# Second attention: k projections written to the PSUM bank of output and routing, the router's logits one double step later

## The reference

```python
x = x + attn_a(layernorm(x), ...)   # 16 heads of 8, unit-norm q and k
x = x + ffn(layernorm(x), ...)      # 8 experts, top 2, capacity 384
x = x + attn_b(layernorm(x), ...)   # 16 heads of 64, position bias, output projection
x = x + ffn(layernorm(x), ...)

# attn_b, the part at issue
q = (h @ Wq).reshape(B, S, 16, 64)
k = (h @ Wk).reshape(B, S, 16, 64)
v = (h @ Wv).reshape(B, S, 16, 64)
probs = softmax(einsum('bqhd,bkhd->bhqk', q, k) / 8 + position_bias)
y = einsum('bhqk,bkhd->bqhd', probs, v).reshape(B, S, 1024) @ Wo

# ffn, its router
probs = softmax(layernorm(x) @ w_router)      # 8 experts
gate, expert = top_k(probs, 2)                # then the place of each token in its expert's rows
```

## Time and profile before

| what | us |
|---|---|
| median of 3 runs | 1679.59 |
| lowest and highest | 1674.07, 1686.88 |
| the profiled execution | 1677.58 |
| its span, first to last instruction | 1675.9 |
| PE busy | 1346.1 (80%) |
| ACT busy | 923.5 (55%) |
| DVE busy | 879.9 (53%) |
| POOL busy | 522.0 (31%) |

### The profile page before, as it was taken

How to read it: one execution, slowest core, us unless ns; L and a number is a source line. 1 busy time by engine, 2 the same in 40 slices (tenths; PEclk the granted TensorE clock), 3 DMA queues, 4 the chain that set the end, 5 groups by cost and what they waited for, 6 DMA issues and landing times. The chain is left out here.

```text
span 1675.9 us, 22605 instructions
## 1 busy us (share of the span) xinstructions
PE 1346.1 (80%) x6711; PEld 596.6 (36%) x6711; DVE 879.9 (53%) x2700; ACT 923.5 (55%) x1844; POOL 522.0 (31%) x789
## 2 busy tenths in 40 slices
PE   2388988887629179999999999999999999997374
PEld 1123333332117023343343343343433433432253
DVE  2445556553311046657667657667577576674211
ACT  0277777776404047656666656666566666564031
POOL 4100222222224413233423433422433334224235
PEclk9699999999859679999999999999999999998687
DMA  3335555556129213333323333323333232333062
GB/s 71 82 83 124 114 117 116 114 119 127 22 76 310 27 41 100 96 87 111 94 82 108 108 94 109 105 78 97 94 108 95 74 107 84 91 101 95 7 153 24
DMA packets 126889, 161.22 MB, mean 96 GB/s; under 512 B 36414, under 2 KB 80909, under 8 KB 126768
## 3 DMA queue, kind: packets, MB, share of 16 engines
q1 hardware_dynamic: 99376, 119.80, 27.5%
q0 software_dynamic: 27392, 39.98, 10.6%
HBM read 61.75 MB, written 36.09 MB: 58 GB/s over the span
## 5 line engine op out<-in xcount | busy, mean ns | idle before, releaser
L1247 POOL DMA_DIRECT2D crossed<-blocks x512 | 252.3, 501 | 609.4 <-DVE blocks L1514 543.8
L1503 DVE CUSTOM_DVE_ANT_0 tile<-s_ps,bias 128x512 f32<-128x512 f32 x512 | 331.2, 684 | 79.7 <-PE s_ps L1313 49.2
L1431 ACT ACTIVATE tile<-tile,low 128x512 f32<-128x512 f32 x512 | 363.2, 715 | 2.2 <-DVE low L1503 2.2
L632 ACT ACTIVATE probs_a<-score_ps,gbound 128x1024 f32<-128x1024 f32 x256 | 268.3, 1114 | 134.2 <-PE score_ps L861 134.1
L1423 ACT ACTIVATE pT<-p_ps 128x512 f32<-128x512 f32 x256 | 152.3, 595 | 269.0 <-PE p_ps L1321 267.3
L1313 PE MATMUL s_ps<-kT,qT 64*128 64x512 f32 x1024 | 255.1, 616 | 0.0
L1336 PE MATMUL o_psb<-pT,v_b 128*64 128x512 f32 x512 | 237.0, 606 | 6.8 <-DMA crossed<-blocks 6.8
L1336 PE MATMUL o_psb<-crossed,v_b 128*64 128x512 f32 x512 | 237.0, 606 | 0.0
L1321 PE MATMUL p_ps<-ident,tile 128*128 128x128 f32 x1024 | 164.6, 283 | 23.0 <-ACT pT L1423 22.9
L1321 PEld LDWEIGHTS p_ps<-ident,tile 128*128 128x128 f32 x1024 | 107.2, 140 | 207.9 <-issue 110.8
L1514 DVE STREAM_TRANSPOSE blocks<-tile 128x512 f32<-128x512 f32 x256 | 180.9, 707 | 0.3 <-ACT tile L1431 0.3
(11 more groups left out here) (153 smaller groups left out, 1484.9 us busy)
## 6 DMA issues: line engine op xcount, KB each, us to landing
crossed<-blocks SPq DMA_DIRECT2D x512, 64.0 KB, 2.6
crossed<-blocks POOLq DMA_DIRECT2D x512, 64.0 KB, 2.4
inv_row<-inv_rows SPq DMA_DIRECT2D x128, 128.0 KB, 2.9
k_stack<-k_parts SPq DMA_DIRECT2D x96, 96.0 KB
q_stack<-q_parts SPq DMA_DIRECT2D x96, 96.0 KB
bias_skew<-bias_rows SPq DMA_DIRECT2D x8, 1024.0 KB, 12.5
w_f<-in_w SPq DMA_DIRECT2D x32, 256.0 KB, 5.5
bias<-bias_skew SPq DMA_DIRECT2D x16, 448.0 KB, 12.4
```

Source lines behind the costliest of these rows:

```text
L632: nc.scalar.activation(probs[q % 2][:, c % 4, :], score_ps[c % 2][:, :], ACT.Exp, bias=gbound[:, :]).then_inc(p_ready.sem, 1)
L1247: pool.dma_start(strip_to(n, a, m), strip_from(n, a, m)).then_inc(crossed_sw[n % 2], 16)
L1431: nc.scalar.activation(tile[k % RING][s][:, :], tile[k % RING][s][:, :], ACT.Exp, bias=low[n % 2][:, s, i:i + 1], scale=-1.0, accum_out=su ...
L1503: nc.vector.tensor_tensor_reduce(out=tile[k % RING][s][:, :], in0=s_ps[k % 2][s][:, :], in1=bias[:, h, off:off + S], scale=1.0, scalar=3.0e38,
```

## The change

In the second attention k projections are written to `r_ps` instead of `m_ps`, and ACT copies them from there. The k projection no longer waits for the copy of q. The q projection and the v projections wait for the last q copied (odd counts of `qk_ready`), not for k. Since `r_ps` now has more users, waits are added on PE: k of pair 0 waits for PLACE of the batch two back, k of pair 3 for the residual, k of pairs 5 and 6 for TURNED and SHIFTED, and the output projection, the router's turn, logits and counts wait for k copies of the next batch. In `ROUTE` `logits` and `shift` go from 24 to 25, `exps` from 25 to 26, `pick` from 26 to 27; the rest stays. Numbers of instructions are the same.

```diff
@@ -1140,8 +1140,8 @@
         def tiles(t):
             return t.rearrange("p (t e) -> p t e", e=E_N)
 
-        ROUTE = dict(stats=20, rows=22, turn=(23, 1), copy=23, logits=(24, 1), shift=24,
-                     exps=25, pick=26, runs=28, counts=(29, 1), take=29, address=30)
+        ROUTE = dict(stats=20, rows=22, turn=(23, 1), copy=23, logits=(25, 1), shift=25,
+                     exps=26, pick=27, runs=28, counts=(29, 1), take=29, address=30)
         R_STEPS = range(20, 31)
 
         def since(eng, signal, b, k):
@@ -1289,19 +1289,25 @@
                 if m == 0:
                     wait(pe, xT_ready, b, 1)
                 else:
-                    wait(pe, qk_ready, b, {1: 2, 3: 4, 4: 6, 5: 8, 6: 10, 7: 12}.get(m, 2))
+                    wait(pe, qk_ready, b, {3: 3, 4: 5, 5: 7, 6: 9, 7: 11}.get(m, 1))
                     wait(pe, v_ready, b, m)
                 i, half = m % TB, m // TB
                 nc.tensor.matmul(m_ps[:, :], xT[:, i * P:(i + 1) * P], wv[:, half * S:(half + 1) * S],
                                  start=True, stop=True).then_inc(v_ps.sem, 1)
 
             def project(b, n, part):
-                if part == 1:
-                    wait(pe, qk_ready, b, 2 * n + 1)
+                if part == 0:
+                    wait(pe, v_ready, b, {0: 1, 1: 3, 2: 4, 3: 5, 4: 6, 5: 7, 6: 8, 7: 8}[n])
+                    since(pe, qk_ready, b, 2 * n - 1)
                 else:
-                    wait(pe, v_ready, b, {0: 1, 1: 3, 2: 4, 3: 5, 4: 6, 5: 7, 6: 8, 7: 8}[n])
                     since(pe, qk_ready, b, 2 * n)
-                nc.tensor.matmul(m_ps[:, :], (wq, wk)[part][:, n * P:(n + 1) * P], xT[:, :],
+                    if n == 0 and b >= 2:
+                        wait(pe, r.step, b - 2, r.PLACE)
+                    if n == 3 and b >= 1:
+                        wait(pe, res_done, b - 1, 1)
+                    if n in (5, 6) and b >= 1:
+                        wait(pe, r.step, b - 1, {5: r.TURNED, 6: r.SHIFTED}[n])
+                nc.tensor.matmul((m_ps, r_ps)[part][:, :], (wq, wk)[part][:, n * P:(n + 1) * P], xT[:, :],
                                  start=True, stop=True).then_inc(qk_ps.sem, 1)
 
             def scores(b, k):
@@ -1339,7 +1345,9 @@
 
             def output(b):
                 wait(pe, ctx_ready, b, PAIRS)
-                if b >= 1:
+                if b + 1 < B:
+                    wait(pe, qk_ready, b + 1, 6)
+                else:
                     wait(pe, r.step, b - 1, r.PLACE)
                 for i in range(TB):
                     for n in range(PAIRS):
@@ -1377,11 +1385,11 @@
 
             def routing(b, d, part):
                 if (d, part) == ROUTE["turn"]:
-                    r.turn(pe, b, turned, lambda: wait(pe, res_done, b, 1))
+                    r.turn(pe, b, turned, lambda: wait(pe, qk_ready, b + 1, 10) if b + 1 < B else wait(pe, res_done, b, 1))
                 elif (d, part) == ROUTE["logits"]:
-                    r.logits(pe, b, logits, lambda: None)
+                    r.logits(pe, b, logits, lambda: wait(pe, qk_ready, b + 1, 12) if b + 1 < B else None)
                 elif (d, part) == ROUTE["counts"]:
-                    r.counts(pe, b, counts, lambda: None)
+                    r.counts(pe, b, counts, lambda: wait(pe, qk_ready, b + 1, 16) if b + 1 < B else None)
 
             for d in range(LEAD, LAST):
                 step(0, d, d >= FIRST)
@@ -1412,7 +1420,7 @@
                 if part == 0:
                     since(act, s_ready, b, 4 * n - 4)
                 wait(act, qk_ps, b, 2 * n + part + 1)
-                nc.scalar.activation((qT, kT)[part][n % 2][:, :], m_ps[:, :], ACT.Copy,
+                nc.scalar.activation((qT, kT)[part][n % 2][:, :], (m_ps, r_ps)[part][:, :], ACT.Copy,
                                      scale=(-1.0 / math.sqrt(DH), 1.0)[part]).then_inc(qk_ready.sem, 1)
 
             def copy_pT(b, k):
```

## The result

The changed kernel takes 1624.62 us (median of 4 runs, 1623.1 to 1627.13), beside it the kernel before 1678.3 us (median of 4). The ratio is 0.9675, with a 95% interval of 0.9635 to 0.9716. The profiled execution took 1624.89 us, where that of before took 1677.58: 52.7 us less. The direction was right, the size was too small.

A forecast was written before the change was run, and what follows sets the result against it. PE was taken to bound the second attention, busy 94.25 of 100 us. Gains of 37.2 + 2.1 + 2.7 = 42.0 us gave 1635.6 us from the profiled 1677.6, 1637.6 us against the median; range 1627 to 1652 us.

The forecast's parts named there:

- I take 0.60 for a k projection.: Second attention, PE: each of 62 k projections no longer waiting for q's copy gains 0.60 us, together 37.2 us.
- 1.13 against 1.02: Lengths in us of k and q projections on PE; the 0.11 us difference entered only the upper bound, 62 x 0.71.
- The first lap: Start of the second attention: three waits of 0.69 us on PE go, 2.1 us gained.
- Logits: Router's logit matmuls one double step later: the second turn's 0.39 us wait for ACT goes in 7 laps, 2.7 us.
- Pick: DVE's pick in an odd double step delays lowest 2.1 us, covered, 0 us; rival (10%): not covered, 15 us back, 1652 us.
- ACT: ACT's k copy and exps move forward with PE; nothing new waits, 0 us, with 3.4 us of cover.
- transfers: Crossings issued by POOL: pair 5's transposes end 2.1 us later, 4.8 us of room remain before values, 0 us.
- guards: Added PE waits around r_ps are satisfied when reached, 0 us; rival (2%): k projections wait for DVE, 1708 us.
- The crossing of d = 12: POOL's transfer in double step 12, issued 0.70 us after the block transposes' end before, expected 2.1 us later, at 1040.98.
- The crossing of d = 10: POOL's transfer in double step 10, issued only at 1027.46 before, with DVE in layernorm rows and pick.
- Single matmul latency: Skill rule, (398 + N) / 2.4 ns for a lone matmul: 0.17 us per k projection, 10.5 us on top, not booked.
- bound of 49 us: Upper bound of the whole gain: 44.0 for k projections plus 2.1 for the first lap plus 2.7 for logits, giving 1631 us.

The follow-up runs named there:

- e5: Kernel before, with only the k projections of pairs 0 and 1 of the first batch in the new bank: 1672.19 us beside 1677.1, ratio 0.9975.
- e9: Changed kernel with the router's double steps as before (the bank alone), rerun on another chip: 1668.13 us beside 1723.68, ratio 0.9683.
- e7: Changed kernel with the router's exp back at 25 and pick at 26: 1621.78 us, ratio 0.9663 to the kernel before.
- e2: Kernel before with only the router's double steps moved (25, 25, 26, 27), k projections in the old bank: 1725.64 us beside 1719.14, ratio 1.0039.
- e3: Changed kernel, but each k projection, in its new bank, waits for the copy of q as before: 1727.41 us beside 1719.14, ratio 1.005.
- e4: Kernel before with only the waits of values moved in front of the second turn: 1720.99 us beside 1719.14, ratio 1.0014.
- e10: Same kernel as e3 (new bank, old wait for q's copy), rerun on another chip: 1731.94 us beside 1723.68, ratio 1.0053.
- e11: Same kernel as e4 (kernel before, values' waits moved forward), rerun on another chip: 1724.57 us beside 1723.68, ratio 0.9997.
- e1: Changed kernel with the router's double steps as before (the bank alone): 1663.49 us beside 1719.14, ratio 0.9679.

## Why the prediction was wrong

The mechanism was right: PE is the limit, the wait for `qT` was on its path 64 times, nothing took its place, and no guard binds (no k projection waits for DVE in the changed kernel). What it had no place for is the clock in the first lap. The step that failed is the price of the removed waits: two terms of the sum were too small, and a third a little.

- **"I take 0.60 for a k projection."** It is 0.73 to 0.74. From the second turn to values it is 2.15 us in the kernel before (1023.02 to 1025.17) and 1.42 in the changed one (0.46 from the turn at 970.79 to the k projection, 0.96 from there to values at 972.21). Of the difference to 0.60, 0.03 us lie in front of the k projection: what follows a second turn can start 0.46 to 0.47 us after it, and the 0.49 that I took stands behind a first turn. The other 0.10 us is the k projection's own, 1.06 us to values before and 0.96 us after. I had this number as a bound (1.13 against 1.02 in the earlier trace rows) and threw it out, because from the k projection to the logits it was 0.96 us. That was a wrong reading of the earlier trace rows: the logits, records of 8 columns, take the delay over. They took 0.88 us there, but in the changed kernel the second turn to scores is 1.35 us with them (991.97 to 993.32) and 0.56 without (966.53 to 967.09), so they cost 0.79. The sum of both distances was what to compare, or any other k projection of the same trace, which has values behind it at once. 62 x 0.735 us are 45.6, not 37.2.
- **The first lap, "2.1 us".** It is 6.0: 12.6 less nine k projections of 0.735, of which e5 shows 5.4. I counted the idle time and not the difference of starts (2.9 us in e5), and did not ask what a denser start does to the granted clock, although PE stands at 0.50 there (2.5 us in e5).
- **Logits, "7 laps x 0.39 = 2.7 us".** The wait went as said, but by the starts it is 7 x 0.47 = 3.3 us, the same error as with k. That the logits may not stay behind the k projection once it writes `r_ps` was not seen: e9 shows that the move is worth 1.7 us a lap, as part of the change.
- **What it comes to.** 45.6 + 6.0 + 3.3 us, and 0.9 us of the last lap that nobody forecast (its values wait 5.9 us for a crossing, before 6.8), are the 55.8 us of the stage. Less the 3.1 us lost outside it they are the 52.7 us between the profiled executions; the sum said 42.0. Without that loss the time would have lain still further below the range.
- **Pick, "0 us on the path", and "before, that would have hit PE at the k projection".** Both right, by e7 and e2.
- **ACT, transfers, guards, "0 us".** Right. The crossing of d = 12 is issued at 1014.07, 0.69 us behind DVE's last block transpose, and values of d = 14 start at 1024.79 without a wait. The crossing of d = 10, which the prediction saw late "with DVE in layernorm rows and pick", is issued at 1001.59, still 2.85 us behind the last block transpose, although pick no longer stands there; so pick isn't what holds it. What does is open.
- **The Trainium skill, "TensorE: Matmul & The Clock Gate", section "Single matmul latency".** I set aside its rule that a matmul standing alone pays for more than its columns, with an estimate of 10.5 us on top. For the k projection's own length I took nothing, the page's formula gave 0.17 us, and 0.10 us came. With the 10.5 us the sum would have been 52.5 us, next to the 52.7 measured, but by luck: 62 x 0.10 us are 6, and the rest came from the first lap and the other terms. The rows point to the weight load behind it and not to the drain.
- **The range.** Its lower end lay 11 us under the forecast. The bound of 49 us for the gain would have been 1631; I had widened it for the runs' spread only. That bound has 0.71 us for a projection, close to what it is; what it lacks above all is the first lap, and nothing in the range stood for a change of the clock.

## What to carry to other kernels

Where an engine that sets the pace waits for a hand-over, the gain of removing it is the difference of starts over the whole place, from the last operation that doesn't change to the first one behind it, and not the idle time; here 0.73 us for a wait shown as 0.47, 1.03 for one shown as 0.78, 0.47 for one shown as 0.39. A small operation next in line can hide part of the cost in its own length. And a wait that is removed may have been what made another operation's lateness matter: judge moves and waits together.

## What was not expected of the hardware

PE's granted clock rose from 0.50 to 1.00 nearly 8 us sooner when three hand-overs of 0.7 us in its first 20 us were gone (e5), and that was worth about as much as the waits, 2.5 us beside 2.9. How much sooner varies between traces; e3 rose early with two of them in place.

On two of the three chips the kernel before took 1719 and 1724 us. In the kernels that wait for q (e2, e3, e4, e10, e11) the first three whole laps took 123 to 128 us and later ones 118 to 120. ACT's copies there were idle up to 4.8 us at a time, for which the profile names `remote` as the releaser, a name that stands at no ACT record of any trace from the other chip or of before and after. e1 has such times too, up to 4.1 us, e9 only up to 0.9 us; both, with the bank alone, kept laps of 113.2 to 114.6 us. What `remote` was, and why it cost less with the new bank, stays open.
